# Attention on rows split into fp16 halves, z products ahead of the scan sum, negations on VectorE and ScalarE, and shorter routing chains

## The chip, the cores and the metric

The kernel runs on one core of a Trainium2 chip. The metric is the device time of one launch in microseconds; the median of three runs stands for the kernel. A profiled execution gives the trace, in which PE is TensorE (PEld its weight loads), DVE VectorE, ACT ScalarE, POOL GpSimd and SP SyncE.

## What is computed

Sixteen images of 96 x 96 x 3 become 36 patches and a class row each (37 rows of 256), 128 text rows are appended (165 in all), and two layers follow, each with an attention-like mixer and a mixture of experts, with layer norms and residual sums in f32.

```python
h = _L0_tok_ref(x, ...)                        # patches -> 16 x 37 x 256
h = jnp.concatenate([h, txt], axis=1)          # 16 x 165 x 256
h = h + _L0_attn_ref(_layernorm(h), ...)       # selective scan y, times gelu(z), times W_out
h = h + _L0_ffn_ref(_layernorm(h), ...)        # 8 experts in 4 groups, one group, two experts
h = h + _L1_attn_ref(_layernorm(h), ...)       # rope, causal softmax, one head of 256
h = h + _L1_ffn_ref(_layernorm(h), ...)        # 4 experts, top 2, gelu
# _L1_attn_ref
Q = _rope(x @ Wq.T + bq); K = _rope(x @ Wk.T + bk); V = x @ Wv.T + bv
A = softmax(where(causal, Q @ K.T / sqrt(256), -inf)); return (A @ V) @ Wf.T + bf
# _L1_ffn_ref: the expert sums need c_sum = sum over e of (gelu(b1) @ w2 + b2)
```

## The kernel before

Each engine has one list of instructions that it works off in order, written out by hand; semaphores join the lists. The residual rows stay in SBUF as 16 text tiles of 128 rows and 6 image tiles of three images (111 rows) each, 22 in all.

*Layer 0.* After the patches, TensorE makes three z products (`z_matmul`, two tiles each), then the routing terms, then 60 products on constants that only keep its clock (`keep_clock`), the first output product, and the sum over the scan (`scan_sum`), which waits for the scan on VectorE. From there a z product and an output product (`o_matmul`) alternate, and VectorE adds each output to the rows (L2677) and takes its statistics. Z results go through three PSUM banks to ScalarE's gelu.

*Expert weights of layer 0.* They lie in 24 chunks of 1024 columns. A casting DMA writes the fp16 high half of four chunks at a time; an engine then writes the negated high half into the place of the low half; an accumulating DMA of three chunks adds the f32 weights, so that the low half is left. POOL negates six chunks itself (L2150) and issues all these DMAs, ScalarE negates 18 beside its gelus (L2281).

*Routing* (`positions`, for both layers). On VectorE a chain of small dependent steps, each waiting for the one before, counts tokens per expert and gives each token a slot; TensorE multiplies one-hot matrices (`pe_slots`) to give the source row of each slot (L762) and its destination (L768). POOL gathers the stored rows (L1107, L1311) and adds results back with indirect DMAs. In VectorE's list the experts of lone tiles (L752 to L757) stand between the one-hot matrices and the sources.

*Experts.* Rows and weights are split in fp16 halves; each product is three fp16 products. These stages are left as they are.

*Attention of layer 1* works in f32, one batch after another. TensorE's list in batch b is the following, and `text(b + 2)` waits for ScalarE's normalised rows:

```python
scores(b, slot)
if b < BATCH - 1: project(b + 1, 1 - slot)
if b: values(b - 1, 1 - slot)
if b < BATCH - 2: text(b + 2, slot)
transpose_p(b)
if b < BATCH - 1: text_values(b + 1, 1 - slot)
if b % PER == PER - 1: image_values(b // PER + 1)
```

VectorE's list in batch b is the maxima of the scores, the rotation of the queries of b + 1 (`rope_of(b + 1, 0)`, L1832 and L1834), the reciprocal of the sums, the rotation of the keys, and the addition of the results of b - 1. POOL's list in batch b is the two sums of the rotation (`rope(b + 1)`, L1767), the copy of the image rows of b + 2 (L1762) and the addition of a bias row (L1771). ScalarE's list is the exponents of b, the normalised rows of b + 2 (`norm`, L2171), copies out of PSUM, and a negation of a chunk of layer 1's weights. `scores(b + 1)` (L1540) waits for `rope(b + 1)`. `project` is 8 f32 products with 165 columns (L1513), `text_values` 2 with 264 columns (L1521), `text` 2 transposes (L1501). The f32 products appear in the trace as two instructions each.

*Second routing.* TensorE makes the bias products of four experts (`bias_out`, L1463) and, a second time, their sum over all experts (`biases_sum`, 4 x 24 products, L2002), the last 24 of them after the first transposes of the gathered rows (`meanwhile`).

Of the kernel before, what the change touches and what calls it, by code (L numbers as in the profile page):

```python
# [17 lines left out]
P = 128  # L18
# [6 lines left out]
KC = D // P  # L25
# [52 lines left out]
W0C, CAST, ADDED = XW0 // CW, 4, 3  # L78
BY_ACT = range(6, W0C)
NEGATED = (0, 2, 2, 2, 2, 2, 2, 2, 2, 2, 0)  # L80
# [98 lines left out]
def build(nc, txt, patches, wtok, cols, rows_a, consts, pe_table, wsmall, w0, wattn, rows_f, w1, wsmall1,  # L179
          b2rows, out):  # L180
    with ExitStack() as ctx:
# [145 lines left out]
        xTi = rx.take([KC, IT, P])  # L327
        xTb = rx.take([2, KC, SEQ])
# [13 lines left out]
        rsum = rx.take([2, 2])  # L342

# [26 lines left out]

        def w0_source(first, n):
            return w0[:, first * CW:(first + n) * CW].rearrange("p (c n) -> p c n", n=CW)
# [23 lines left out]
        w0_cast = [sem(f"w0_cast{i}") for i in range(W0C // CAST)]  # L396
        own_negated = sem("own_negated")
        w0_negated = sem("w0_negated")
# [93 lines left out]
        p_exp = sem("p_exp")  # L492
        p_normed = sem("p_normed")
# [7 lines left out]
        rest_ready = sem("rest_ready")  # L501
# [25 lines left out]
        Z_BANKS = (2, 3, 1)  # L527
# [152 lines left out]
        def positions(dve, chain, choices, tiles, done, inrow, intile, pairs, singles):  # L680
# [3 lines left out]
            odd, paired, moved = (sm[:, 12 + 4 * i:16 + 4 * i] for i in (0, 2, 3))  # L684
            so = sm[:, 16:20] if done else sm[:, 28:32]
            if choices == 2:
                chain.link(nc.vector.tensor_tensor(hot, oh[:, 0], oh[:, 1], ALU.add))
                chain.link(nc.vector.tensor_tensor(hot, hot, over(k_valid, 4), ALU.mult))
            else:
                chain.link(nc.vector.tensor_tensor(hot, oh[:, 0], over(k_valid, 4), ALU.mult))  # L690
            nc.vector.tensor_copy(ohb[:, :, :], hot).then_inc(choice_ready, 1)
# [3 lines left out]
            nc.vector.tensor_copy(flat(before_), PS[:, 7, 0:4 * NT])  # L695
            chain.link(nc.vector.tensor_copy(flat(total), PS[:, 7, 128:128 + 4 * NT]))
            chain.link(nc.vector.tensor_tensor_scan(flat(upto), k_reset, flat(total), 0.0, ALU.mult, ALU.add))
# [4 lines left out]
            tl, st, sl = sm[:, 0:4], sm[:, 4:8], sm[:, 8:12]  # L702
# [4 lines left out]
            chain.link(nc.vector.tensor_scalar(sl, st, float(T1), None, ALU.mult))  # L707
            chain.link(nc.vector.tensor_tensor(odd, odd, tl, ALU.subtract))
            chain.link(nc.vector.tensor_scalar(paired, tl, float(T1), None, ALU.mult))
            chain.link(nc.vector.tensor_tensor_scan(so[:, 1:4], onesf[:, 0:3], odd[:, 0:3], 0.0, ALU.mult, ALU.add))  # L710
            chain.link(nc.vector.tensor_scalar(so, so, -1.0, float(2 * pairs + singles - 1), ALU.mult, ALU.add))
            chain.link(nc.vector.tensor_tensor(moved, sl, paired, ALU.add))
            chain.link(nc.vector.scalar_tensor_tensor(out=moved, in0=so, scalar=float(P), in1=moved, op0=ALU.mult,
                                                      op1=ALU.subtract))
            chain.link(nc.vector.tensor_tensor(upto, upto, total, ALU.subtract))
            chain.link(nc.vector.tensor_tensor(before_, before_, upto, ALU.add))
            chain.link(nc.vector.tensor_tensor(upto, before_, over_tokens(paired), ALU.is_ge))
            chain.link(nc.vector.tensor_tensor(upto, upto, over_tokens(moved), ALU.mult))
# [8 lines left out]
            chain.link(nc.vector.tensor_tensor(slots_of, slots_of, k_far.unsqueeze(1).broadcast_to([P, choices, NT]), ALU.add))  # L727
            row_of, first_of = low7[:, 0:choices, :], high7[:, 0:choices, :]
            chain.link(nc.vector.tensor_copy(pos[:, 0:choices, :], slots_of))
# [21 lines left out]
            alone = slice(2 * pairs, 2 * pairs + singles)  # L751
            chain.link(nc.vector.tensor_scalar(sg_, k_slot[:, alone], so[:, 1:2], None, ALU.is_le))  # L752
            for g in (2, 3):
                chain.link(nc.vector.scalar_tensor_tensor(out=sg_, in0=k_slot[:, alone], scalar=so[:, g:g + 1],
                                                          in1=sg_, op0=ALU.is_le, op1=ALU.add))
            chain.link(nc.vector.tensor_tensor(sf[:, alone], sf[:, alone], sg_, ALU.min))
            nc.vector.tensor_copy(slote[:, 0:tiles], sf).then_inc(slots_ready, 1)  # L757
# [10 lines left out]
            nc.vector.tensor_copy(dest[:, 0:tiles], to).then_inc(dest_ready, 1)  # L768
# [4 lines left out]
        def pe_gram(pe):  # L773


            for e in range(G0 * E0):
                for u in range(2):
                    pe.wait_ge(w0_cast[(3 * e + u) // CAST], 16)
# [347 lines left out]
        def pe_experts1(pe, meanwhile):  # L1126
# [42 lines left out]
            def tile(i, slot, j):  # L1169
                w_ = weights(i)  # L1170
                if known(i, 0):
                    transpose_x(0, 0, 0)
                    meanwhile()
# [29 lines left out]
        def act_experts1(act):  # L1203
# [27 lines left out]
            def tile(i, slot, j):  # L1231
                if known(i, 0):
                    split_x(0, 0)
                    act.wait_ge(c_psum, 3)
                    nc.scalar.activation(csum, PS[:, 6, 0:D], ACT.Copy).then_inc(c_copied, 1)
# [9 lines left out]
        def dve_experts1(dve, chain):  # L1245
# [37 lines left out]
            def tile(i, slot, j):  # L1283
# [5 lines left out]
                if known(i, 0):  # L1289
                    dve.wait_ge(c_copied, 2)  # L1290
                    nc.vector.tensor_tensor(rest1[:, :, :], csum.unsqueeze(1).broadcast_to([P, E1, D]), rest1[:, :, :],
                                            ALU.subtract).then_inc(rest_ready, 1)
                if known(i, 1):
                    dve.wait_ge(rest_ready, 1)
# [85 lines left out]
        def pe_rest(pe):  # L1380
# [6 lines left out]
            pe.wait_ge(w0_added, 16 * W0C // ADDED)  # L1387
# [91 lines left out]
        def pe_attention(pe):  # L1479

            def image(n):
                pe.wait_ge(xi_ready, n + 1)
                for k in range(KC):
                    ins = nc.tensor.transpose(PS[:, IMAGE_BANK[n], k * P:(k + 1) * P], xnF[:, 2 + n, k * P:(k + 1) * P],
                                              k_ident)
                ins.then_inc(xi_tr, 1)

            def beside(n):

                pe.wait_ge(xi_ready, n + 1)  # L1490
                for k in range(KC):
                    ins = nc.tensor.transpose(PS[:, 7, BESIDE + k * P:BESIDE + (k + 1) * P], xnF[:, 2 + n, k * P:(k + 1) * P],
                                              k_ident)
                return ins

            def text(b, slot):
                pe.wait_ge(xn_ready, NF + b + 1)
                if not known(b, 0):
                    pe.wait_ge(xTb_copied, b)
                for k in range(KC):  # L1500
                    ins = nc.tensor.transpose(PS[:, 7, k * P:(k + 1) * P], xnF[:, slot, k * P:(k + 1) * P], k_ident)  # L1501
# [4 lines left out]
            def project(b, slot):  # L1506
# [3 lines left out]
                for bank, w_, done in ((0, wq, q_psum), (1, wk, k_psum)):  # L1510
                    for m in range(KC):
                        for k in range(KC):
                            ins = nc.tensor.matmul(PS[:, bank, m * SEQ:(m + 1) * SEQ], w_[:, k, m * P:(m + 1) * P],  # L1513
                                                   xTb[:, slot, k, :], start=(k == 0), stop=(k == KC - 1))
                    ins.then_inc(done, 1)

            def text_values(b, slot):

                wait_from(pe, v_copied, b)
                for k in range(KC):  # L1520
                    ins = nc.tensor.matmul(PS[:, 2, 0:PAYV], xTb[:, slot, k, IMG:SEQ], wvx[:, k, :],  # L1521
                                           start=(k == 0), stop=(k == KC - 1))
                ins.then_inc(v_psum, 1)

            def image_values(n):
# [5 lines left out]
                for k in range(KC):  # L1531
                    ins = nc.tensor.matmul(PS[:, 5, 0:PAYV], xTi[:, k, n, :], wvx[:, k, :], start=(k == 0), stop=(k == KC - 1))
# [79 lines left out]
            keep_clock(8, 5)  # L1612
            project(0, 0)
            keep_clock(16, 5)
            text_values(0, 0)
# [24 lines left out]
        def act_attention(act, roots, normal):  # L1640
            def image(n):
                act.wait_ge(xi_tr, n + 1)
                nc.scalar.activation(xTi[:, :, n, :], PS[:, IMAGE_BANK[n], 0:KC * P].rearrange("p (k r) -> p k r", k=KC),
# [1171 lines left out]
```

## Time and profile before

| | us |
|---|---|
| median of 3 runs | 774.8 (773.57 to 776.81) |
| the profiled execution's own time | 773.13 |
| its span, first to last instruction | 771.3 |
| PE busy | 712.1 (92%) |
| DVE busy | 445.7 (58%) |
| ACT busy | 370.5 (48%) |
| POOL busy | 293.1 (38%) |

The span is read by the stages: front and scan to 100 us, first routing to 138, experts of layer 0 to 338, preparation of attention to 357, attention to 462, second routing to 504, experts of layer 1 to 756, output. The page's line of the granted clock is given in tenths of full speed, which is 2.4 GHz; 0.5 is 1.2 GHz.

### The profile page before, as it was taken

How to read it: one execution, taken by the hardware profiler on the slowest of the kernel's cores; microseconds unless marked ns; L12 is line 12 of the kernel's file. 1: busy time of each engine (PE TensorE's matmuls, PEld its weight loads, DVE VectorE, ACT ScalarE, POOL GpSimd, SP SyncE). 2: the span in 40 equal slices, each digit the busy share in tenths (PEclk: the TensorE clock that was granted, in tenths of full speed). 3: DMA queues.
4: the chain of work that ended last, by engine and by line, in shares of the span. 5: the costliest groups of instructions: out<-in, count | busy, mean ns of one | idle time of the engine just before them, and what ended most of it. 6: DMA issues, size and time to landing. Idle time of an engine off the chain costs nothing.

```text
span 771.3 us, 18265 instructions
## 1 busy us (share of the span) xinstructions
PE 712.1 (92%) x6093; PEld 621.8 (81%) x6094; DVE 445.7 (58%) x1218; ACT 370.5 (48%) x871; POOL 293.1 (38%) x259
## 2 busy tenths in 40 slices
PE   5989985999999999989899999799999999999981
PEld 5768974889888897668789988688888888888871
DVE  5897678344444443437897778745454555555440
ACT  6898745433344433333667656343433444343430
POOL 3348101222333224114455430226555655564331
PEclk9999996999999999999999999899999999999996
DMA  9896998114122112137741279112333332332235
GB/s 273 189 211 81 140 165 265 43 29 120 28 41 41 27 22 35 22 67 193 151 56 18 39 94 316 32 36 43 45 51 55 43 46 48 55 48 41 36 36 154
DMA packets 42214, 66.22 MB, mean 86 GB/s; under 512 B 3680, under 2 KB 29264, under 8 KB 41616
## 3 DMA queue, kind: packets, MB, share of 16 engines
q0 software_dynamic: 22304, 39.19, 33.5%
q1 hardware_dynamic: 19664, 25.93, 10.6%
q8 instruction: 35, 0.57, 0.3%
q10 hardware_dynamic: 192, 0.38, 0.1%
q14 instruction: 19, 0.16, 0.1%
HBM read 65.80 MB, written 23.35 MB: 116 GB/s over the span
## 4 chain that ended last, share of the span: by engine, by line
PE 74%; DVE 13%; ACT 4%; DMA 3%; issue 2%; POOL 1%; POOLq 0%; SPq 0%; DVEq 0%
PE PS L1146 16%; PE PS L1159 15%; PE PS L853 14%; PE PS L890 8%; PE PS L1513 3%; PE PS L868 3%; PE PS L2451 3%; PE PS L2465 2%; ACT Y L2171 2%; PE PS L1540 1%; PE PS L1131 1%; PE PS L1463 1%; DMA xs<-Y 1%; DMA X<-in_w_dram 1%; PE PS L1521 1%
## 5 line engine op out<-in xcount | busy, mean ns | idle before, releaser
L1159 PE MATMUL PS<-X 128*128 x720 | 125.8, 273 | 1.9 <-ACT X L1228 1.9
L1325 POOL DMA_INDIRECT sum<-X,dest x45 | 89.7, 1993 | 96.2 <-ACT X L1228 80.5
L1146 PE MATMUL PS<-X 128*128 128x256 f16 (+1 forms) x768 | 122.7, 265 | 0.7 <-issue 0.7
L1218 ACT ACTIVATE X<-PS,X 128x256 f32<-128x256 f32 (+1 forms) x192 | 72.6, 461 | 103.5 <-PE PS L1146 100.4
L853 PE MATMUL PS<-Y,X 128*128 128x256 f16 x960 | 108.1, 273 | 0.5 <-DVE Y L1022 0.5
L853 PEld LDWEIGHTS PS<-Y,X 128*128 x960 | 93.9, 98 | 11.5 <-issue 0.7
L1146 PE MATMUL PS<-X,Y 128*128 128x256 f16 (+1 forms) x384 | 100.2, 264 | 0.0
L1159 PE MATMUL PS<-Y,X 128*128 x360 | 98.2, 273 | 0.0
L1117 POOL DMA_INDIRECT sum<-Y,dest x24 | 38.6, 1610 | 111.4 <-DVE Y L1050 107.8
L1146 PEld LDWEIGHTS PS<-X 128*128 x768 | 71.7, 97 | 10.6 <-issue 1.3
L1159 PEld LDWEIGHTS PS<-X 128*128 128x128 f16 x720 | 70.4, 98 | 11.1 <-issue 3.0
L1036 DVE TENSOR_TENSOR Y<-PS,Y 128x512 f32<-128x512 f32 x48 | 33.2, 691 | 68.6 <-PE PS L853 48.3
L1311 POOL DMA_INDIRECT X<-xs,source x45 | 45.5, 1010 | 71.2 <-DVE source L762 38.7
L890 PE MATMUL PS<-X,Y 128*128 x576 | 67.5, 273 | 2.0 <-DVE Y L1041 2.0
L890 PEld LDWEIGHTS PS<-X,Y 128*128 128x128 f16 x576 | 56.2, 98 | 8.9 <-issue 2.5
L1277 DVE SCALAR_TENSOR_TENSOR PS<-PS,hscale,X 128x256 f32<-128x256 f32 x45 | 20.0, 488 | 74.9 <-PE PS L1159 74.9
L1269 DVE SCALAR_TENSOR_TENSOR X<-X,hscale 128x1024 f16<-128x1024 f32 (+1 forms) x48 | 58.4, 1217 | 1.7
L974 ACT ACTIVATE Y<-Y,hscale 128x512 f16<-128x512 f32 x40 | 28.9, 722 | 55.7 <-DVE Y L1036 55.7
L1107 POOL DMA_INDIRECT Y<-xs,source x24 | 23.6, 984 | 67.3 <-DMA xs<-Y 33.0
L1041 DVE SCALAR_TENSOR_TENSOR Y<-Y,hscale 128x512 f16<-128x512 f32 x40 | 30.4, 760 | 31.6 <-ACT Y L974 31.6
L1767 POOL TENSOR_TENSOR X<-X 128x330 f32<-128x330 f32 x32 | 28.4, 886 | 50.5 <-DVE X L1834 50.5
L966 ACT ACTIVATE Y<-PS 128x512 f32<-128x512 f32 x48 | 28.3, 589 | 35.8 <-PE PS L853 24.9
(408 smaller groups left out, 1385.3 us busy)
## 6 DMA issues: line engine op xcount, KB each, us to landing
X<-in_w_dram POOLq DMA_DIRECT2D x10, 1024.0 KB, 16.2
X<-in_w_dram POOLq DMA_DIRECT2D x8, 768.0 KB, 15.4
sum<-h SPq DMA_DIRECT2D x2, 2048.0 KB, 15.1
Y<-in_w_dram POOLq DMA_DIRECT2D x4, 1024.0 KB, 11.3
xs<-Y SPq DMA_DIRECT2D x2, 1040.0 KB, 6.2
xs<-Y SPq DMA_DIRECT2D x2, 1032.0 KB, 8.8
h<-in_txt_dram SPq DMA_DIRECT2D x2, 1024.0 KB, 16.5
Y<-in_patches_dram SPq DMA_DIRECT2D x3, 672.0 KB, 7.7
```

What stands on the lines that cost most here:

```text
L853: ins = nc.tensor.matmul(PS[:, 2 * u + half, c * T1:c * T1 + tokens], w_[:, at_:at_ + P], x_[:, slot, k, 0:tokens], start=(n == 0), stop=( ...
L890: ins = nc.tensor.matmul(PS[:, Y_BANKS[s], a * D:(a + 1) * D], h_[:, s, c, a * P:(a + 1) * P], w_[:, at_:at_ + D], start=(c == 0 and n == ...
L974: nc.scalar.activation(to, whole, ACT.Copy, scale=hscale[:, 0:1]).then_inc(hT_hi, 1)
L1036: nc.vector.tensor_tensor(whole, up, gate, ALU.mult).then_inc(h_ready, 1)
L1041: nc.vector.scalar_tensor_tensor(out=low, in0=whole, scalar=hscale[:, 0:1], in1=high, op0=ALU.mult, op1=ALU.subtract).then_inc(hT_lo, 1)
L1117: nc.gpsimd.indirect_dma_start(out=sum0, out_offset=bass.IndirectOffsetOnAxis(ap=dest[:, i:i + 1], axis=0), in_=ybuf[:, u % 2, i - first0( ...
L1146: ins = nc.tensor.matmul(PS[:, 2 * s + c // 2, (c % 2) * T1:(c % 2) * T1 + tokens], part[:, off:off + P], x_[:, slot, k, 0:tokens], start= ...
L1159: ins = nc.tensor.matmul(PS[:, 4 + a, 0:D], h_[:, s, c, a * P:(a + 1) * P], part[:, off:off + D], start=(s == 0 and c == 0 and n == 0), st ...
L1218: ins = nc.scalar.activation(hh1[:, s, c, 0:tokens], PS[:, 2 * s + c // 2, (c % 2) * T1:(c % 2) * T1 + tokens], ACT.Gelu, bias=bias1[:, sl ...
L1269: nc.vector.scalar_tensor_tensor(out=lo_, in0=act_, scalar=hscale[:, 2:3], in1=hi_, op0=ALU.mult, op1=ALU.subtract).then_inc(h1_lo, 1)
L1311: nc.gpsimd.indirect_dma_start(out=x1in[:, u % 2, n - first_tile(u), :], out_offset=None, in_=xs1, in_offset=bass.IndirectOffsetOnAxis(ap= ...
L1325: nc.gpsimd.indirect_dma_start(out=sum1, out_offset=bass.IndirectOffsetOnAxis(ap=dest[:, i:i + 1], axis=0), in_=y1buf[:, u % 2, i - first_ ...
```

## The change

1. *Attention.* The projections of queries, keys and values take rows and weights as two fp16 halves, each f32 product being replaced by three fp16 products. Text rows are split by POOL (`split_text`: a rounding and a subtraction), image rows by VectorE (`norm_image`: two more steps), the query and key weights by ScalarE and VectorE, the value weights by POOL (`split_values`). Transposes are of fp16 halves, four in place of two. `text(b)` on TensorE now waits for `xn_split`. Scores, softmax and values stay in f32.
2. *Layer 0.* `z_matmul(3)` and `z_matmul(4)` stand ahead of the scan sum, with 8 clock-keeping products in place of 60; four z banks at the start; the scan sum goes to another bank and waits for the second gelu; each output product comes a pair earlier against the z products.
3. *Negations of layer 0's weights.* VectorE does 12 (four ahead of its additions of a bias row, eight beside its first four sums), ScalarE 12, POOL none; the accumulating DMAs are of four chunks, six in place of eight; the first casting DMA is issued before a wait of POOL. In layer 1 ScalarE's negations start at b = 2, some batches have two, and POOL's three accumulating DMAs in the loop come at b = 6, 9 and 12.
4. *Routing.* Steps are merged or read PSUM directly; the lone tiles' experts move behind the destinations.
5. *Second routing.* `biases_sum` is gone; VectorE sums the experts' bias products with four additions (`rest_of_outputs`) ahead of the experts; clock-keeping products stand at four places in place of one.

```diff
-BY_ACT = range(6, W0C)
-NEGATED = (0, 2, 2, 2, 2, 2, 2, 2, 2, 2, 0)
+NEGATED1 = (0, 0, 1, 1, 1, 1, 1, 2, 1, 1, 2, 1, 1, 2, 1, 0)
+ADD_IN = (6, 9, 12)
+BY_DVE, BY_ACT = (0, 2, 4), (1, 3, 5)
+BESIDE_GELU = (0, 0, 4, 2, 2, 2, 2)
+BESIDE_SUMS = (2, 2, 2, 2)
...
             def text(b, slot):
-                pe.wait_ge(xn_ready, NF + b + 1)
+                pe.wait_ge(xn_split, b + 1)
...
-                for k in range(KC):
-                    ins = nc.tensor.transpose(PS[:, 7, k * P:(k + 1) * P], xnF[:, slot, k * P:(k + 1) * P], k_ident)
+                for q in range(2 * KC):
+                    ins = nc.tensor.transpose(turned2[:, q * P:(q + 1) * P], xn2[:, slot, q // KC, q % KC * P:(q % KC + 1) * P],
+                                              ident2)
...
                         for k in range(KC):
-                            ins = nc.tensor.matmul(PS[:, bank, m * SEQ:(m + 1) * SEQ], w_[:, k, m * P:(m + 1) * P],
-                                                   xTb[:, slot, k, :], start=(k == 0), stop=(k == KC - 1))
+                            for n, (wh, xq) in enumerate(((0, k), (0, KC + k), (1, k))):
+                                ins = nc.tensor.matmul(PS[:, bank, m * SEQ:(m + 1) * SEQ], w_[:, wh, k, m * P:(m + 1) * P],
+                                                       xTb[:, slot, xq, :], start=(k == 0 and n == 0),
+                                                       stop=(k == KC - 1 and n == 2))
...
+            def split_text(b):
+
+                pool.wait_ge(xn_ready, NF + b + 1)
+                nc.gpsimd.tensor_copy(xn2[:, b % 2, 0, :], xnF[:, b % 2, :]).then_inc(own_rounded, 1)
+                pool.wait_ge(own_rounded, b + 1 + (b > 0))
+                nc.gpsimd.tensor_tensor(xn2[:, b % 2, 1, :], xnF[:, b % 2, :], xn2[:, b % 2, 0, :], ALU.subtract)\
+                    .then_inc(xn_split, 1)
...
+            split_text(0)
             image(0)
+            pool.wait_ge(prep_copied, 4)
+            split_values()
+            split_text(1)
             image(1)
             rope(0)
...
                 if b < BATCH - 1:
                     rope(b + 1)
                 if b < BATCH - 2:
+                    split_text(b + 2)
                     image(b + 2)
                     bias(b + 2)
...
             for i in range(3):
                 z_matmul(i)
             prepare_routes()
-            keep_clock(60, 7)
+            z_matmul(3)
+            keep_clock(8, 5)
             pe.wait_ge(base_ready, 1)
             o_matmul(0)
+            z_matmul(4)
             scan_sum()
-            for i in range(3, NT // 2):
+            o_matmul(1)
+            for i in range(5, NT // 2):
                 z_matmul(i)
-                o_matmul(i - 2)
-            for i in range(NT // 2 - 2, NT // 2):
+                o_matmul(i - 3)
+            for i in range(NT // 2 - 3, NT // 2):
                 o_matmul(i)
...
-            biases_sum(0, True, False)
-            biases_sum(1, False, False)
             biases_rest()
-            keep_clock(85, 3)
+            pe.wait_ge(rows_known, 2)
+            keep_clock(50, 3)
             pe_slots(pe, 1, TOPK * NT, SLOT1, inrow1, intile1)
-            biases_sum(2, False, False)
+            keep_clock(40, 3)
             pe.wait_ge(slots_ready, 2)
             pe.wait_ge(dest_ready, 2)
             pe_scale(pe, 1)
             pe.wait_ge(c_copied, 1)
-
-            def meanwhile():
-                biases_sum(3, False, True).then_inc(c_psum, 1)
-            pe_experts1(pe, meanwhile)
+            keep_clock(45, 3)
+            pe_experts1(pe)
```

## Rows read from the trace of the kernel before

**Rows 1.** The page, part 4: the chain that ended last, by engine

```profile
PE 74%; DVE 13%; ACT 4%; DMA 3%; issue 2%; POOL 1%; POOLq 0%; SPq 0%; DVEq 0%
```

**Rows 2.** Timeline (start us, us, instructions), PE, one batch of attention (b = 10)

```profile
424.35 1.09 PE L1540 MATMUL PS<-X 128*128 128x165 f32 x8
425.28 2.49 PE L1513 MATMUL PS<-X,Y 128*128 128x165 f32 x16
427.61 0.60 PE L1562 MATMUL PS<-X 128*128 128x260 f32 x2
...
428.48 0.38 PE L1501 MATMUL PS<-cst,X 128*128 128x128 f32 x2
428.70 0.27 PE L1550 MATMUL PS<-cst,X 128*128 128x128 f32 x1
...
429.03 1.06 PE L1521 MATMUL PS<-Y,X 128*128 128x264 f32 x4
430.23 1.20 PE L1540 MATMUL PS<-X 128*128 128x165 f32 x8
```

**Rows 3.** Timeline, DVE, the same batch: first and last step of the rotations

```profile
426.69 0.39 DVE L1832 SCALAR_TENSOR_TENSOR X<-PS,ccols,Y 128x165 f32<-128x165 f32 x1 [0.56 <-PE PS L1513]
...
428.83 0.38 DVE L1834 SCALAR_TENSOR_TENSOR X<-PS,ccols,Y 128x165 f32<-128x165 f32 x1
```

**Rows 4.** Timeline, POOL, the same batch: second rotation sum, bias row

```profile
429.29 0.88 POOL L1767 TENSOR_TENSOR X<-X 128x330 f32<-128x330 f32 x1 [0.36 <-DVE X L1834]
...
430.32 0.72 POOL L1771 TENSOR_TENSOR h<-h,wsm 128x256 f32<-128x256 f32 x1
```

**Rows 5.** Timeline, PE: scores of b = 0 and of b = 14

```profile
357.69 1.10 PE L1540 MATMUL PS<-X 128*128 128x165 f32 x8
...
448.68 1.20 PE L1540 MATMUL PS<-X 128*128 128x165 f32 x8
```

**Rows 6.** Chain that ended last, in order of time (start us, us), 455 to 512 us

```profile
470.74 3.57 PE PS L790 x64
...
499.83 3.84 PE PS L2002 x24
503.67 2.63 PE PS L1146 x24
```

**Rows 7.** Timeline, POOL, 0 to 140 us: f32 copy, fp16 negations

```profile
25.96 0.61 POOL L2129 COPY Y<-wsm 128x512 f32<-128x512 f32 x1
...
49.95 8.25 POOL L2150 TENSOR_SCALAR X<-X 128x1024 f16<-128x1024 f16 x3 [5.44 <-DVE Y L2607]
```

**Rows 8.** Timeline, PE, 452 to 512 us: products behind two pauses

```profile
488.42 4.46 PE L590 MATMUL PS<-X 128*128 128x138 bf16 x44 [2.02 <-DVE X L742]
...
498.73 1.10 PE L1131 MATMUL PS<-cst,X 128*128 128x128 f32 x4 [2.14 <-DMA X<-xs,source]
```

**Rows 9.** Windows of 2 us: busy of PE, PEld, DVE, ACT, POOL, then PEclk, DMA share, GB/s

```profile
368.00:370.00 2.00, 0.23 (x2) 0.22 (x3) 0.75 (x4) 1.90 (x8) 0.25 (x1) 1.00 1.15 242
...
486.00:488.00 2.00, 0.41 (x8) 0.23 (x5) 2.00 (x3) 1.53 (x3) 0.00 (x0) 1.00 0.00 0
488.00:490.00 2.00, 1.58 (x15) 1.61 (x16) 2.00 (x3) 0.00 (x0) 0.00 (x0) 0.63 0.00 0
```

**Rows 10.** Chain that ended last, in order of time: one z product

```profile
94.67 1.77 PE PS L2451 x16
```

**Rows 11.** Timeline, DVE: ninth sum, sources of layer 0, one-hot scaling, input split

```profile
101.98 0.48 DVE L2677 SCALAR_TENSOR_TENSOR h<-PS,yv,h 111x256 f32<-111x256 f32 x1 [1.64 <-PE PS L2465]
...
131.05 0.18 DVE L762 SCALAR_TENSOR_TENSOR source<-PS,stats 128x24 uint32<-128x24 f32 x1
...
486.00 0.74 DVE L740 TENSOR_SCALAR X<-X,cst 128x2024 bf16<-128x2024 bf16 x1
...
500.50 0.69 DVE L1250 TENSOR_TENSOR X<-PS,X 128x512 f16<-128x512 f32 x1 [4.57 <-ACT X L1207]
```

**Rows 12.** Timeline, POOL: first gather of layer 0

```profile
132.10 1.09 POOL L1107 DMA_INDIRECT Y<-xs,source  x1 [33.03 <-DMA xs<-Y]
```

More of the change, by code:

```diff
@@ L342, in build @@
         rsum = rx.take([2, 2])
+        xn2, xi2 = rx.take([2, 2, D], F16), rx.take([2, 2, D], F16)
+        wqk2 = stage[:, 1, :].bitcast(F16).rearrange("p (h n) -> p h n", h=2)
+        wq2, wk2 = (wqk2[:, :, i * KC * D:(i + 1) * KC * D].rearrange("p h (k n) -> p h k n", k=KC) for i in range(2))
+        wvx2 = wqk.bitcast(F16)[:, 0:2 * KC * PAYV].rearrange("p (h k n) -> p h k n", h=2, k=KC)
+        ident2 = stage[:, 0, CW - P // 2:CW].bitcast(F16)
+        turned2 = PS[:, 7, :].bitcast(F16)
         rg = Region(X, XE)
@@ L767, in positions @@
             dest_of_token(dve, chain, tiles, from_, to, taken)
-            nc.vector.tensor_copy(dest[:, 0:tiles], to).then_inc(dest_ready, 1)
+            chain.link(nc.vector.tensor_copy(dest[:, 0:tiles], to))
+            dve.sem_inc(dest_ready, 1)
+            alone = slice(2 * pairs, 2 * pairs + singles)
+            chain.link(nc.vector.tensor_scalar(so[:, 1:4], so[:, 1:4], -1.0, float(last), ALU.mult, ALU.add))
+            chain.link(nc.vector.tensor_scalar(sg_, k_slot[:, alone], so[:, 1:2], None, ALU.is_le))
+            for g in (2, 3):
+                chain.link(nc.vector.scalar_tensor_tensor(out=sg_, in0=k_slot[:, alone], scalar=so[:, g:g + 1],
+                                                          in1=sg_, op0=ALU.is_le, op1=ALU.add))
+            chain.link(nc.vector.tensor_tensor(sf[:, alone], sf[:, alone], sg_, ALU.min))
+            nc.vector.tensor_copy(slote[:, 0:tiles], sf).then_inc(slots_ready, 1)
         def pe_gram(pe):
@@ L1697, in negate @@
             def negate(b):
-                for n in range(b + 1 if b else 0, min(b + 2, W1W // CW)):
+                for n in range(sum(NEGATED1[0:b]), sum(NEGATED1[0:b + 1])):
                     act.wait_ge(*w1_landed(n * CW // W1N))
@@ L1804, in pool_attention @@
                     image_bias(IMAGE_BIAS.index(b))
-                if b and b % (W1N // CW) == 0:
-                    add(b * CW // W1N - 1)
+                if b in ADD_IN:
+                    add(ADD_IN.index(b))
             add(E1 - 1)
@@ L1987, in act_layer1 @@
                 .then_inc(c_copied, 1)
+            act_rows(act, 1, inrow1)
             act_experts1(act)
@@ L1994, in pe_layer1 @@
             pe.wait_ge(small1_loaded, 16)
-            def biases_sum(e, first, last):
-                for c in range(F1 // P):
-                    off = e * W1N + KC * F1 + c * D
-                    for n, (g_, w_) in enumerate(((gbh, w1h), (gbh, w1l), (gbl, w1h))):
-                        left = g_[:, e * (F1 // P) + c:e * (F1 // P) + c + 1].broadcast_to([P, P])
-                        ins = nc.tensor.matmul(PS[:, 6, 0:D], left, w_[:, off:off + D], start=(first and c == 0 and n == 0),
-                                               stop=(last and c == F1 // P - 1 and n == 2))
-                return ins
             def biases_rest():
@@ L2691, in _ @@
                     add_bout(BATCH, IT)
+                for _ in range(BESIDE_SUMS[i] if i < len(BESIDE_SUMS) else 0):
+                    negate(chunks.pop(0))
                 if i == BATCH // 2 - 1:
```

215 lines of the change are left out of this document (118 added, 97 removed).

## Prediction

> **What bounds the kernel now.** I read the shares of the chain that ended last first: TensorE (PE) carries 74% of the span, VectorE (DVE) 13% [rows 1]. The two expert stages, 138 to 333 us and 504 to 756 us, are gapless PE work that the change doesn't touch, so whatever it brings or costs lies in three stretches: layer 0's z and output products with the first routing (54 to 138 us), attention (340 to 462 us), and the second routing (462 to 504 us). Within attention I then read one undisturbed batch, b = 10, engine by engine [rows 2 to 4], and the distance of the first from the last scores that open a full cycle [rows 5]: 14 cycles in 448.68 - 357.69 = 91.0 us, 6.5 us each. The undisturbed one takes 430.23 - 424.35 = 5.88 us. The remaining 91.0 - 14 x 5.88 = 8.7 us are image products and DVE statistics in some of them. PE looks full in such a cycle, but what ends last is a loop through other engines. Let S be the start of the projections, 425.28 [rows 2]. DVE takes up the rotation of the queries at 426.69, 0.24 us after the first half of the projections (1.17 us), and ends that of the keys at 429.21 [rows 3]; POOL adds from 429.29 to 430.17 [rows 4]; the next scores start at 430.23, released by nothing else. So the loop is scores 0.93, then 4.95 us from S to the next scores, and PE's last piece (the text values, from 429.03 for 0.89) is done 0.3 us before.
>
> **Attention: the new order of waits.** The change takes away PE time. The price of an fp16 product follows from 64 of 128 columns in 3.57 us (56 ns each, own weights for each) and 24 of 256 columns in 2.63 us (110 ns) [rows 6]: 71 ns for 165 columns, some 113 ns for 264. The projections become 24 x 71 ns = 1.71 us instead of 2.33 [rows 2], their first half 0.86 instead of 1.17; the text values 6 x 113 ns = 0.68 instead of 0.89; the four fp16 transposes stay at 0.22 us. The Trainium skill (TensorE: Matmul & The Clock Gate, section Back-to-back issue gap) gives 81 ns to a sustained pair of weight load and 128-column product. The row of 64 says 56 ns, and I go by it; by the page an estimate of the first half is at least 0.97 us, which adds 0.11 us to a cycle and 1.6 us in all.
>
> It also adds a step to POOL, and the place of this step decides. In POOL's list, split_text(b + 2) stands behind rope(b + 1); in PE's list, text(b + 2) waits for that split, and behind text(b + 2) are queued transpose_p(b), text_values(b + 1) and scores(b + 1). In the kernel before, text(b + 2) waited only for ScalarE's normalised rows, ready long before. Now scores(b + 1) can't start at the end of POOL's rotation any more: first come POOL's rounding and subtraction, then PE's transposes and the values. The subtraction of 256 elements costs 0.72 us as in [rows 4]. A rounding of 256 elements from f32 to f16 has no row on POOL; below it is the f32 copy of 512 elements (0.61 us, so 0.3 for half of it), above it the f16 TENSOR_SCALAR of 1024 at 8.25 / 3 = 2.75 us (0.69 for a quarter) [rows 7]; I take 0.4, nearer to the copy, and 0.05 for the wait between the two. So the loop after is, from S:
> - first half of the projections 0.86, to DVE 0.24, both rotations with the quotients between them 429.21 - 426.69 = 2.52, to POOL 0.08, sum 0.88: 4.58;
> - split 0.4 + 0.05 + 0.72 = 1.17, to PE 0.05: 5.80;
> - transposes 0.22, transposes of p 3 x 0.11 = 0.33, text values 0.68, scores 0.93: 7.96.
>
> Against 5.88 this is 2.08 us more in each of the 14 cycles that have a split (b = 0 to 13), 14 x 7.96 = 111.4 in all. Four image products (0.68 each) and four more image transposes (0.22 each) now lie behind the split too: +3.6. DVE's statistics are covered by the longer loop except in the two cycles with a full Newton chain, and ScalarE's three double negations may delay an exponent: +2. Sum 117 against 91.0: **+26 us**. The last cycle has no split and gains from the shorter projections: -0.5. Ahead of the first scores, two image splits on DVE and the split of two text rows and of the value weights on POOL stand in line before project(0) and rope(0): about 1.3 us later. The split of the query and key weights is hidden, since both engines wait there for the transposed weights.
>
> **The clock.** With 1.71 + 0.88 of values behind S, PE has no work from S + 2.6 to S + 5.8: 3.2 us of idle time in one piece in each cycle. Twice in this trace the engine stood still for about 2 us: 2.02 before 488.42 and 2.14 before 498.73 [rows 8]. After the first the clock granted fell from 1.00 to a mean of 0.63 in the next stretch of 2 us, so to the 1.2 GHz level in most of it [rows 9]; the second shows in the durations below. A pause of 1.8 us in 368 to 370 left it at 1.00 [rows 9]. A pause of 3.2 us is longer than the one that cost the clock, so I expect the fall in most cycles. What it costs: 24 products of 256 columns took 3.84 us after the second pause, and 2.63 us at 2.4 GHz [rows 6]: 1.2 us. The ends are 0 (the 368 us row) and 2.16 us (everything behind the pause, scores included, at half speed). 14 x 1.2 = **+17 us**, between 0 and +30.
>
> **Layer 0.** Two z products, 1.77 us each [rows 10], move from behind the scan sum to before it, where clock-keeping products stood: -3.5. Their order also brings the last three output products together, so that DVE's wait of 1.64 us before the ninth [rows 11] goes: -1.6. Negations: POOL's six go. DVE gets twelve; 16-bit in and out costs 0.74 us for 2024 elements [rows 11], so about 0.4 for 1024. Eight lie two by two in waits of 1.6 us like that one; four stand ahead of the step that prepares the scan, where DVE waits for ScalarE in part: +0.5, between 0 and 1.6. Then the routing: five short DVE steps (copies, a multiply, an add, a rounding) leave the chain, and six on the lone tiles move behind the destinations; at some 0.2 us each, like the step at 131.05 that gives the sources [rows 11], these come 2.3 us earlier besides. Gathering waits today for the stored rows (132.10 [rows 12]); with six adds issued sooner, I expect the store to come as early as the sources. Sum about **-7**, with -4 if the store stays the later one and -8 at best; who is late next is PE's scale with its clock-keeping products, some 0.2 us behind.
>
> **Second routing.** The sums of four experts' bias products, 96 in all, leave PE. Only the last 24 stood on the chain: 3.84 us from 499.83 on [rows 6]. In their place stand 18 clock-keeping products (1.0 us at 56 ns), and what ends last is then the input split, done at 500.50 + 0.69 = 501.19 [rows 11], 1.4 us after the transposes: -2.4. DVE's shorter chain brings the sources about 1.4 us earlier; the four DVE adds that replace the products fit while it waits for the gathered rows. Clock-keeping products ahead of the gathered rows can use up some of it. Together **-4**, between -2 and -5.
>
> **Sum.** -7 + 1.3 + 26 + 17 - 0.5 - 4 = +33 (32.8). The span of 771.3 becomes 804; the profiled run itself, 773.13, lies 1.7 under the median 774.8, to which I add the rounded 32: **806 us**.
>
> **Rivals.**
> - *The clock holds.* For it: the row at 368 us, and that the pause lies between two stretches of dense work. Against it: the row at 488 us, with a shorter pause. Without the 17: **790 us**.
> - *All behind the pause at half speed*, and the rounding at 0.69: 14 x (0.96 + 0.3) = 17.6 more: **823 us**. For it: two of two long pauses cost the clock at once; against it: there, part of what followed was fast again.
> - *Faster: the split costs PE no wait.* The place is PE's wait at text(b + 2). If the split were done by the time PE gets there, S + 2.6, for which POOL has idle time ahead of the rotation sums, the loop would be 5.88 - 0.31 = 5.57; 14 of them, with today's extras of 8.7 less 0.7 for smaller products, make 86, that is -5; without a pause the clock holds: 774.8 - 7 + 1.3 - 5 - 0.5 - 4 = **760 us**. The other parts sum to -10.2, so it decides from (91.0 + 10.2) / 14 = 7.23 us a cycle, extras of 0.4 included, or a loop of 6.8, and with the clock up: nearly all of the split's 1.17 us would have to vanish. Against it: POOL's list is in order, and the rotation stands ahead.
> - *The change does less than it says*, for instance if the projections don't get shorter by 0.3 us in the first half: +4, inside the forecast.
>
> **How the numbers follow.** Forecast (loop of 8 us and more, clock falling) 0.56, 806; clock holds 0.20, 790; half speed throughout 0.10, 823; split hidden 0.11, 760; all cancelled within 0.5% 0.03. The range takes in the bounds of the clock and of the rounding: 786 to 824; outside it remain the hidden split and little else. A difference of 0.5% (3.9 us) is about what a measurement of this kernel can tell from none: faster 0.11, same 0.03, slower 0.86.
>
> **What will show it.** In the profile after: starts of scores 8 us apart or more for b = 0 to 13 and some 5.5 for the last; before the text transposes an idle time of about 3 us each, released by POOL's subtraction; a PEclk below 1.0 in the slices of attention; at PE the last z product ahead of the eighth output product; sources of both layers earlier by the amounts above. I am wrong if PE's idle time in these batches stays under 1 us, or if it is released by ScalarE.

## The result and the profile after

The changed kernel takes 819.0 us (816.69 to 821.19) against 774.5 us (773.57 to 776.81) for the kernel before in the same comparison: a ratio of 1.0577, with a 95% interval of 1.0557 to 1.0597. The forecast was 806 us with a range of 786 to 824, so sign and range held and the size was 13 us short. The profiled execution took 819.52 us, its span is 817.7.

Five marks of the trace, read in the same views of both kernels, split the span into stages; the column "added" says how much longer each stage got (us):

| up to | before | after | added | forecast |
|---|---|---|---|---|
| first expert product of layer 0 | 138.51 | 139.25 | +0.7 | -7 |
| scores of b = 0 | 357.69 | 362.32 | +3.9 | +1.3 |
| scores of b = 14 | 448.68 | 498.13 | +44.8 | +26 and +17 |
| first expert product of layer 1 | 503.67 | 550.20 | -2.9 | -0.5 and -4 |
| end | 771.3 | 817.7 | -0.1 | 0 |

The loss is attention, and it came nearly as worked out (44.8 for 43). What the forecast missed lies around it: 7.7 us of gain in layer 0, 2.6 us of loss ahead of attention, 1.6 us of gain behind it. These three and the 1.8 us of the loop are 13.7 us, the whole difference between the forecast span (804) and the measured one.

The scores of b = 0 and b = 14 on TensorE in the changed kernel (start us, us, instruction), to be set beside [rows 5]:

```profile
362.32 2.07 PE L1557 MATMUL PS<-X 128*128 128x165 f32 x8 [1.93 <-POOL X L1789]
...
498.13 1.09 PE L1557 MATMUL PS<-X 128*128 128x165 f32 x8
```

The 14 cycles take 135.8 us, 9.7 each. One of them, b = 10, on TensorE (compare [rows 2]):

```profile
460.69 1.47 PE L1557 MATMUL PS<-X 128*128 128x165 f32 x8
461.99 1.90 PE L1526 MATMUL PS<-X,stage 128*128 128x165 f16 x24
...
464.21 0.60 PE L1580 MATMUL PS<-X 128*128 128x260 f32 x2
467.69 0.40 PE L1512 MATMUL PS<-stage,X 128*128 128x128 f16 x4 [2.88 <-POOL X L1796]
...
468.25 1.50 PE L1536 MATMUL PS<-Y,X 128*128 128x264 f16 x6
469.55 2.01 PE L1557 MATMUL PS<-X 128*128 128x165 f32 x8
```

and on POOL (compare [rows 4]):

```profile
464.42 0.88 POOL L1789 TENSOR_TENSOR X<-X 128x330 f32<-128x330 f32 x1 [3.35 <-DVE X L1878]
465.66 0.88 POOL L1789 TENSOR_TENSOR X<-X 128x330 f32<-128x330 f32 x1 [0.36 <-DVE X L1878]
466.49 0.39 POOL L1794 CAST X<-X 128x256 f16<-128x256 f32 x1
466.96 0.67 POOL L1796 TENSOR_TENSOR X<-X 128x256 f16<-128x256 f32 x1
```

TensorE stands still for 2.88 us ahead of the text transposes, and POOL's subtraction (L1796) releases it. The rounding took 0.39 us (forecast 0.4), the subtraction 0.67 (0.72). From the projections to the text transposes it is 467.69 - 461.99 = 5.70 us; the sum in the prediction said 5.80.

The clock in the same cycle, in stretches of 2 us (busy of PE, PEld, DVE, ACT, POOL, then PEclk, DMA share, GB/s; compare [rows 9]):

```profile
464.00:466.00 2.00, 0.81 (x4) 0.36 (x2) 2.00 (x9) 0.76 (x2) 1.22 (x2) 1.00 1.12 138
466.00:468.00 2.00, 0.31 (x5) 0.32 (x6) 0.74 (x5) 0.00 (x0) 1.92 (x5) 1.00 1.06 136
468.00:470.00 2.00, 2.00 (x13) 1.65 (x12) 0.00 (x0) 1.22 (x5) 0.57 (x1) 0.57 1.10 142
470.00:472.00 2.00, 2.00 (x15) 2.00 (x14) 0.33 (x2) 2.00 (x4) 0.00 (x0) 0.58 0.13 15
```

In this pause the granted clock reads 1.00 (2.4 GHz); it falls to 0.50 (1.2 GHz) about 0.5 us behind it. So the four transposes still run fast here (0.40 us, against 0.61 at 458.32, where the clock was already down), and the six text values take 1.50 us (0.84 in b = 13, at 497.46) and the next eight score instructions 2.01 (1.09).

Layer 0, the chain that ended last, in order of time (start us, us, what):

```profile
109.00 9.84 ACT Y L2213 x20
...
119.43 12.27 DMA xs<-Y
...
136.22 1.12 PE PS L853 x4
137.33 1.92 PE PS L572 x18
139.25 0.85 PE PS L871 x4
```

and the same view of the kernel before:

```profile
113.52 9.84 ACT Y L2171 x20
...
123.37 8.26 DMA xs<-Y
...
138.51 5.41 PE PS L853 x48
```

ScalarE is 4.5 us earlier with the scaled rows, as the forecast had it. But their last store takes 12.27 us in place of 8.26 and lands at 131.70 us, where it landed before (131.63). The sources, at 131.05 before [rows 11], now come at 124.15, on VectorE:

```profile
124.15 0.18 DVE L771 SCALAR_TENSOR_TENSOR source<-PS,stats 128x24 uint32<-128x24 f32 x1
```

Before, POOL's first gather started 1.05 us behind them (132.10 [rows 12]); now it starts 7.8 us behind them, released by the store:

```profile
131.97 1.10 POOL L1125 DMA_INDIRECT Y<-xs,source  x1 [44.22 <-DMA xs<-Y]
```

So nothing of the 4.5 us came through. TensorE now waits 6.46 us for the gathered rows (up to 136.22), and the clock is down behind it (0.50 from 135 to 140 us, 1.00 before): the four transposes take 1.12 in place of 0.67 us, and the 18 clock-keeping products 1.92 us (107 ns each), which is 0.4 us more than the input split behind the transposes needed before. These two are the 0.7 us that were lost.

Ahead of attention, on VectorE and POOL:

```profile
348.23 0.75 DVE L1854 BATCH_NORM_STATS2 stats<-h 128x6 f32<-128x256 f32 x2 [1.14 <-DMA h<-sum]
...
355.08 1.05 DVE L2565 TENSOR_TENSOR rs<-rs 128x17 f32<-128x17 f32 x1
...
358.18 0.29 DVE L1867 CAST X<-X 128x256 f16<-128x256 f32 x1
358.51 0.42 DVE L1868 TENSOR_TENSOR X<-X 128x256 f16<-128x256 f32 x1
```

```profile
354.89 1.21 POOL L1804 TENSOR_TENSOR Y<-Y 128x528 f16<-128x528 f32 x1
```

The first statistics come 209.0 us behind the first expert product (before: 345.93 - 138.51 = 207.4), as VectorE now waits for the rows that SP loads back: +1.6. Two image splits of 0.75 us: +1.5. One VectorE step of 17 elements takes 1.05 us, where the same step took 0.18 at 349.72: +0.9. Together 4.0, for 3.9 measured.

Second routing, the chain in order of time:

```profile
545.73 2.51 PE PS L572 x45
548.24 0.46 PE PS L1149 x4
...
550.20 2.80 PE PS L1164 x24
```

The first gather is issued at 542.09 and, at the 4.15 us that it took before from POOL's start to its landing (494.53 to 498.68), landed at about 546.2. The transposes start 2.0 us later, behind 45 clock-keeping products.

### The profile page after: what moved, and what is told of

It is laid out like the page before. It is cut to its first block, busy times and chain, and to the rows that moved or that the text cites. A ratio compares the mean times of both kernels' runs of the same rounds, so it can differ in the third digit from the quotient of the medians.

```text
span 817.7 us, 18586 instructions
## 1 busy us (share of the span) xinstructions
PE 708.6 (87%) x6229; PEld 618.5 (76%) x6230; DVE 456.8 (56%) x1235; ACT 370.7 (45%) x867; POOL 291.3 (36%) x285
## 3 DMA queue, kind: packets, MB, share of 16 engines
q1 hardware_dynamic: 19664, 25.93, 10.1%
## 4 chain that ended last, share of the span: by engine, by line
PE 72%; DVE 12%; ACT 6%; DMA 4%; POOL 3%; issue 2%; POOLq 0%; SPq 0%; DVEq 0%
PE PS L1164 15%; PE PS L1177 15%; PE PS L871 13%; PE PS L908 8%; PE PS L1526 3%; PE PS L886 3%; PE PS L1557 2%; PE PS L2509 2%; PE PS L1536 2%; PE PS L2495 2%; POOL X L1789 2%; DMA xs<-Y 1%; ACT Y L2213 1%; DVE X L1876 1%; DVE X L1878 1%
## 5 line engine op out<-in xcount | busy, mean ns | idle before, releaser
L871 PEld LDWEIGHTS PS<-Y,X 128*128 x960 | 94.4, 98 | 11.2
L1789 POOL TENSOR_TENSOR X<-X 128x330 f32<-128x330 f32 x32 | 28.2, 882 | 75.5 <-DVE X L1878 75.5
L572 PE MATMUL PS<-onesb 128*128 128x128 bf16 x415 | 31.8, 247 | 16.2 <-DVE rc L747 9.4
```

The lines of the kernel that those rows point to most:

```text
L572: nc.tensor.matmul(PS[:, bank, 0:P], onesb[:, :], onesb[:, :], start=True, stop=True)
L871: ins = nc.tensor.matmul(PS[:, 2 * u + half, c * T1:c * T1 + tokens], w_[:, at_:at_ + P], x_[:, slot, k, 0:tokens], start=(n == 0), stop=( ...
L1789: nc.gpsimd.tensor_tensor(qkT[:, b % 2, i], tcos[:, i], tsin[:, i], ALU.add).then_inc(rope_done, 1)
```

## The experiments

### The place of the split

```diff
                 for b in range(BATCH):
+                if b < BATCH - 2:
+                    split_text(b + 2)
                 if b < BATCH - 1:
                     rope(b + 1)
                 if b < BATCH - 2:
-                    split_text(b + 2)
                     image(b + 2)
```

Alone, this is the first run; the second has in ScalarE's list `norm(b + 2)` ahead of `exps(b)` besides.

> Only POOL's list is changed: split_text(b + 2) ahead of rope(b + 1). ScalarE's rows stay behind the exponents, where they are done 2.4 us after the start of the projections. Theory (place of the split): POOL splits from 2.5 to 3.6 us after that start, TensorE's wait for it shrinks from 2.9 to about 0.9 us, the clock stays up, and the two rotation sums come behind it, the second at 5.35 us: loop 5.4 + 0.93 = 6.35 us, some 95 us between the scores of b = 0 and b = 14, about 778 us in all. Rival (cost of the split itself): above 8.4 us a cycle and 800 us.

Measured: 786.1 us, one execution. 14 cycles in 464.29 - 363.58 = 100.7 us, 7.2 each (95 were expected). A plain cycle takes the 6.4 us that were worked out; b = 2 and b = 6 take 11.2 and 9.6.

```profile
363.58 1.85 PE L1557 MATMUL PS<-X 128*128 128x165 f32 x8 [1.93 <-POOL X L1789]
...
464.29 1.20 PE L1557 MATMUL PS<-X 128*128 128x165 f32 x8 [0.28 <-POOL X L1789]
```

> In POOL's list split_text(b + 2) stands ahead of rope(b + 1), and in ScalarE's list the normalised rows of b + 2 stand ahead of the exponents of b; nothing else differs from the changed kernel. Theory (place of the split): the split is done before TensorE gets to the text transposes, its wait of about 2.9 us per batch goes, and with it the fall of the granted clock. The loop is then that of the rotation, 4.6 us from the projections to the next scores and 0.93 for the scores, 5.6 us; 14 of them with about 8 us of image products and statistics are 86 us in place of 135.8 between the scores of b = 0 and b = 14, and the run takes about 819 - 50 = 769 us. Rival (cost of the split itself, wherever it stands: more POOL work and more TensorE instructions in each batch): the cycles stay above 8.4 us and the run above 800. Second rival: the rows ahead of the exponents delay these and the products behind them, loop about 6.5 us, 95 us in all, 778 us.

Measured: 774.7 us, a ratio to the kernel before of 1.0021 (1.0006 to 1.0036). Scores on TensorE:

```profile
362.12 1.20 PE L1557 MATMUL PS<-X 128*128 128x165 f32 x8 [1.21 <-POOL X L1789]
...
447.94 1.20 PE L1557 MATMUL PS<-X 128*128 128x165 f32 x8
453.59 1.20 PE L1557 MATMUL PS<-X 128*128 128x165 f32 x8 [0.56 <-POOL X L1789]
```

The same work in another order is 44 us faster: the 14 cycles take 91.5 us, and scores are again released by the rotation sum (L1789). So the place of the split is the cause, and the rival (its cost wherever it stands) falls. POOL's order alone brings 35 of the 44 us (the run before this one); ScalarE's order by itself was not run. But 86 were expected. A plain cycle is 5.65 us, nearly as worked out, so the second rival (6.5 us) falls too; the rest, 91.5 - 14 x 5.65 = 12.4 us, is more than the 8.7 before. It sits in cycles with VectorE's image rows, now three steps each: b = 2, 6 and 7 take 10.0, 8.2 and 7.7 us (8.6, 6.8 and 6.0 before). In b = 2 TensorE still waits 1.8 us for the split, and in all three it waits for ScalarE's normalised probabilities, whose exponents wait for VectorE's maxima:

```profile
417.26 0.33 PE L1567 MATMUL PS<-cst,X 128*128 128x128 f32 x1 [1.63 <-ACT X L1691]
```

### The clock

```diff
                 if b < BATCH - 2:
+                    for _ in range(40):
+                        nc.tensor.matmul(PS[:, 4, 3 * P:4 * P], onesb[:, :], onesb[:, :], start=True, stop=True)
                     text(b + 2, slot)
```

> The changed kernel with 40 clock-keeping products of 128 columns on TensorE ahead of each text(b + 2), in a part of PSUM that nothing reads; the split keeps its place. At 56 ns each they fill 2.2 of the 2.4 to 3.2 us that TensorE waits there, so they delay nothing. Theory: the wait stays as the profile of the changed kernel shows it, but the granted clock stays at 1.00, and each cycle loses the part that came from the clock: 14 cycles fall from 135.8 to about 117 us (8.4 us each), and the run takes about 800 us. Rival (the slow products behind the pause have another cause than the pause, or the lower clock costs nothing on the path): the 14 cycles stay within 3 us of 135.8 and the run within 3 us of 819.

Measured: 801.6 us, one execution. A cycle, and the whole of the 14:

```profile
401.09 2.40 PE L1647 MATMUL PS<-onesb 128*128 128x128 bf16 x40
404.14 0.40 PE L1512 MATMUL PS<-stage,X 128*128 128x128 f16 x4 [0.66 <-POOL X L1798]
...
404.71 0.84 PE L1536 MATMUL PS<-Y,X 128*128 128x264 f16 x6
```

```profile
363.75:480.35 116.60, 105.66 (x1290) 98.71 (x1291) 77.70 (x313) 60.22 (x204) 63.78 (x99) 1.00 0.39 62
```

The split still releases the transposes, the clock is 1.00 throughout (0.84 on the mean in the changed kernel), and the cycles fall from 135.8 to 116.6 us. A plain cycle takes 7.88 us, for 7.96 in the prediction's sum. So the 44.8 us are 116.6 - 91.0 = 25.6 for the wait and 19.2 for the clock; the forecast had 26 and 17. The rival (the clock costs nothing on the path) falls.

### The rest of the change alone

Attention as in the kernel before (f32, no split), all else as changed.

> The changed kernel with attention as it was before (f32 projections and values, no splits); layer 0, negations, both routings as changed. Theory: the parts add up as the two traces say, stage by stage: layer 0 and first routing +0.7 us, second routing -2.4 us, attention as before: 774.5 - 1.7 = about 773 us, no difference that can be measured. Rival (interaction): two negations of layer 1's weights in some batches on ScalarE delay exponents in an f32 attention that has no slack for them, 2 to 4 us more: 775 to 777 us.

Measured: 770.3 us, a ratio of 0.9971 (0.9959 to 0.9984). So by the two ratios attention costs 47 us and the rest gains 2.2. On the same chip the changed kernel with the split first took 774.7 us, 4.5 more than the f32 one: with 4.5 of the 41.5 us of TensorE's wait in the 14 cycles left, the split attention doesn't pay here. Whether it would with none left was not run. The f32 cycles:

```profile
361.68 1.10 PE L1550 MATMUL PS<-X 128*128 128x165 f32 x8
...
450.60 1.20 PE L1550 MATMUL PS<-X 128*128 128x165 f32 x8
```

88.9 us for 14, 2.1 less than before. Within these cycles only the places of ScalarE's negations (none in b = 0 and 1) and of POOL's accumulating transfers differ, so the rival (negations delay exponents) falls too. The other stages come to no gain in this profiled execution (771.6 us of span, 771.3 before); it was the longest execution of ten, by 3.6 us over their median, and the stages don't show where the median gains.

### The stores of layer 0

In the changed kernel, from 96 to 114 us (queue: packets, MB, share of 16 engines) the accumulating transfers take most of the engines' time; from 114 to 132 it is SP's queue:

```profile
q0 software_dynamic: 1076, 2.14, 91.6%
q1 hardware_dynamic: 769, 0.79, 15.7%
```

```profile
q1 hardware_dynamic: 4943, 5.00, 88.5%
```

SP's queue has 2816 KB of residual rows ahead of 2838 KB of scaled rows, and of the former only 0.79 MB are through by 114 us. The residual rows aren't needed before 163 us.

```diff
-            for t, n in ((0, BATCH), (BATCH, IT)):
-                ... sp.dma_start(sum0[...], h[...])
             for t, n in ((0, 8), (8, 8), (BATCH, IT)):
                 ... sp.dma_start(xs0[...], pay[...])
+            for t, n in ((0, BATCH), (BATCH, IT)):
+                ... sp.dma_start(sum0[...], h[...])
```

> The changed kernel with one exchange in SP's list: the three stores of the scaled rows (xs), for which the first gather waits, stand ahead of the two stores of the residual rows (sum, 2.75 MB), for which only the first addition of results waits. In the profile of the changed kernel the scaled rows are ready 4.5 us earlier than before, but their last store takes 12.3 instead of 8.3 us and lands at 131.7 us as before. Theory (SP's queue works its stores off in order, and 2 MB of the residual rows are still ahead when the accumulating transfers end at 115 us): the store lands at 125 to 127 us, and the first expert product of layer 0 starts at about 134 instead of 139.3, so the run takes about 814 us. Rival (the accumulating transfers of the expert weights hold the engines until then, whatever the order on SP's queue): the store lands at 131 us or later and the run stays at 819. Second rival: the residual rows then lie beside the first gathers, which take 2 us longer, and half of the gain goes.

Measured: 817.0 us (808.33 to 818.55), a ratio of 1.0524 (1.0461 to 1.0587), which can't be told from 1.0577. The stage can:

```profile
119.50 6.06 DMA xs<-Y
...
127.24 6.55 DMA Y<-xs,source
...
136.12 3.89 PE PS L871 x26
```

The store lands at 125.56 us, as expected from the order on the queue; the gather then takes 6.55 us in place of 2.81, so that 3.1 of 6.1 us are left. The second rival was right about that part.

> The changed kernel with attention in f32 as it was before, and SP's stores of the scaled rows ahead of those of the residual rows. Theory (order on SP's queue): 5 us below the same kernel without the exchange, 770.3 - 5 = about 765 us. Rival (accumulating transfers): 770 us.

Measured: 766.8 us, ratio 0.9917 (0.9898 to 0.9937): 3.5 us below the same kernel without the exchange, or 4.2 by the two ratios, as the two ran on different chips; 5 were expected.

> The kernel before with the exchange of stores alone. There the scaled rows land at 131.63 us and the sources of the first gather come at 131.23 us, so two waits end nearly together. Theory (two limits in series: the change shortened the chain to the sources, the store kept the gather where it was): the store lands 4 us earlier, the first gather starts at most 0.4 us earlier, and as it then has the residual rows beside it, the first expert product comes 1 to 3 us later than at 138.5: 774 to 777 us. Rival (the store alone was the limit in both kernels): the first product comes 3 us earlier, 771 us.

Measured: 775.5 us, ratio 1.0023 (1.0008 to 1.0039): slower by 0.2%, as expected. The chain:

```profile
131.31 0.20 DVE source L762
...
133.76 4.62 DMA Y<-xs,source
...
140.57 1.48 PE PS L853 x12
```

In the kernel before, the sources were as late as the store. The exchange alone gains nothing there, and the longer gather costs 2 us. Two limits ended together; the change moved one, the exchange the other, and in layer 0 each alone is worth nothing. By the ratios the change without the split attention gains 2.2 us, the exchange alone loses 1.8, and both together gain 6.4.

### The clock-keeping products of the second routing

```diff
-            keep_clock(45, 3)
+            keep_clock(8, 3)
             pe_experts1(pe)
```

> The changed kernel with 8 instead of 45 clock-keeping products ahead of the first transposes of layer 1's experts. In its profile these 45 start behind a wait of 2.3 us and take 2.5 us, and the transposes start at 548.2, about 2 us after the gathered rows landed. Theory (the products themselves are what ends last): the transposes start when the rows land, 2 us earlier against the one-hot products; as the clock is then still down, they take 1.1 instead of 0.5 us, and the first expert product comes about 1.4 us earlier against the one-hot products. Rival (the products pay for themselves): the expert's first 24 products then run at half clock, 3.8 instead of 2.8 us, and the second unit starts no earlier than now. In the time of the run that is 819 against 818, so the stage tells it.

Measured: 820.4 us, one execution. Counted from the one-hot products (535.61 here, 536.27 in the changed kernel), the transposes come at 10.1 instead of 12.0 us, but the second unit at 554.25 - 535.61 = 18.6 instead of 553.43 - 536.27 = 17.2:

```profile
546.21 1.24 DVE X L2115
...
549.25 4.57 PE PS L1164 x24
```

VectorE's four additions for the bias products, ending at 547.45, now hold up the input split, and the first 24 products take 4.57 us in place of 2.80. Here the products paid for themselves.

> As the kernel with f32 attention and the exchanged stores, and with 8 instead of 45 clock-keeping products ahead of the transposes of layer 1's experts; with f32 attention those 45 took 4.1 us, all of it at half clock. Theory: 2 to 3 us less than with 45, about 762 us. Rival (the products pay for themselves): 765 us or above.

Measured: 764.4 us, ratio 0.9896 (0.9868 to 0.9925). The interval overlaps with the kernel with 45, so the expected 2 to 3 us are not shown by the times. From the last scores to the second unit it is 48.2 us against 50.2, and the first 24 products took 2.80 us in both, so in these two profiled executions the products did not pay. The same 45 products took 2.51 us in the changed kernel, 3.78 with the exchanged stores and 4.09 with f32 attention (91 ns each, so not all of it at half clock, as was expected: that is 107); what sets this was not found, and the question of their best number stays open.

### A faster kernel

The kernel of the run before, in which SP in addition waits for the first gathers:

```diff
+            sp.wait_ge(x_in[0], 32)
+            sp.wait_ge(x_in[1], 32)
             for t, n in ((0, BATCH), (BATCH, IT)):
                 ... sp.dma_start(sum0[...], h[...])
```

> The kernel with f32 attention, exchanged stores and 8 kept products; in addition SP issues the stores of the residual rows only when the first four gathers have landed (they are needed by about 159 us). With the stores exchanged, the scaled rows landed at 124.8 us, but the first gather then took 6.2 us in place of 2.8. Theory (the residual rows share the engines with the gather): the gather takes 2.8 to 3 us again, the first expert product of layer 0 starts at 132 to 133 instead of 135.8, and the run takes about 761 us. Rival (something else slows the gather, such as the last accumulating transfers): it still takes 6 us, and the run stays at 764.

Measured: 761.4 us (760.27 to 766.29), ratio 0.9847 (0.9831 to 0.9862): the fastest, 1.5% below the kernel before. Gathers from 120 to 150 us (KB each, median us from issue to landing), first without that wait, then with it:

```profile
Y<-xs,source POOLq DMA_INDIRECT x7, 5.1
```

```profile
Y<-xs,source POOLq DMA_INDIRECT x7, 2.8
```

The residual rows were what slowed the gather. The profiled execution is the longest of the five, its sources came 3.4 us later than in the run before (127.44 for 124.05), and its first expert product (136.92) says nothing on the 132 to 133 expected, which stay unshown.

## Why the prediction was right, and where it was short

- **What bounds attention, and the loop after.** Right, step by step: the wait for POOL's subtraction, 5.70 us for 5.80 from the projections to the transposes, and +25.6 for +26 at full clock. The order in POOL's list was the cause, as moving it showed.
- **The clock.** Right in the mechanism: the clock fell in 11 of the 14 cycles ("in most cycles"), and taking the fall behind the pause of 2.02 us at 488 us rather than none behind that of 1.8 us at 368 us was the right choice of row. That the size is so near, 19.2 us for 17, is partly luck: the sum had 14 falls of 1.2 us, and the runs show 11, of 1.7 us on the mean.
- **Layer 0: the step that failed.** "With six adds issued sooner, I expect the store to come as early as the sources", and with it -4 "if the store stays the later one". The first part of the sum held (4.5 us to the scaled rows for 3.5 + 1.6 - 0.5 = 4.6, and 6.9 us to the sources). But the bound was wrong: it took the store's length as fixed and let its end move with its start. The DMA engines were full from 80 to 130 us in both kernels (share 1.03 to 1.09 in every stretch of 5 or 10 us) with the same transfers, so with the stores in this order the end did not move (131.69 for 131.63 us); with the rows stored first it came at 125.56. The bound should have been 0, which is what the 4.5 us were worth. That the last add was issued 12 us sooner (86.0 for 97.8) brought nothing: the adds now took up to 30.9 us to landing, before up to 19.0.
- **Ahead of attention.** A term too small (3.9 for 1.3). The two image splits were there (1.5); the wait for the rows (1.6) and the slow step (0.9) were not.
- **Second routing.** -2.4 for -4, with the -0.5 of the last cycle as forecast. The sources came 1.4 us earlier as said (0.3 us between the one-hot products and them, 4.81 for 5.11, and 1.1 us ahead of the one-hot products). The step "what ends last is then the input split, 1.4 us after the transposes" holds, but the transposes themselves were held by 45 products, which was named and not priced; and the additions do not quite "fit while it waits for the gathered rows", as the run with fewer products shows.
- **The rival at 760.** Its mechanism was built (the split mostly hidden), and the run took 775. The loop came 5.5 us longer than its 86 through VectorE's image rows, and it carried the same -7, +1.3 and -4.
- **The sum.** It comes to 32.8 us and was added to 774.8 as 32. With 32.8 the forecast is 807.6, so 1.6 of the 13 us is a slip of the adding.

## What to carry to other kernels

A step added to an in-order list delays all that waits behind it on other engines: the same split made 14 cycles 45 us longer behind the rotation, 10 us longer ahead of it, and 0.5 us longer when its input was moved ahead too. So ask of each added step whether its inputs are ready before those of its neighbours. Where the DMA engines were already full, a store issued 4 us sooner ended no sooner; what moved its end by 6 us was what stood ahead of it in its queue. So store first what somebody waits for. Where two waits end together, shorten both or neither.

## What was not expected of the hardware

The price of a pause is paid by what stands behind it, and not each pause has the same price. In b = 10 the granted clock reads 1.00 in a pause of 2.9 us and falls when work has resumed (1.00 from 466 to 468 us, 0.57 from 468 to 470). Of the 14 pauses of the changed kernel's loop, five (2.44 to 4.12 us long) end with the clock at 0.50 already and the transposes at 0.61 us; behind six (2.44 to 2.89 us) it falls 0.5 to 1.5 us after the transposes start; behind three (2.85 to 2.90 us, ahead of 381.17, 439.24 and 496.89) it stays at 1.00 up to the next pause. So in this range the length of a pause alone doesn't tell what it costs.

A VectorE step of 17 elements took 1.05 us instead of 0.18. It starts at 355.08 and ends at 356.13, while POOL's subtraction runs from 354.89 to 356.10. The Trainium skill (SBUF — State Buffer, section Who interferes with whom) says that a VectorE instruction with two SBUF inputs contends with a GpSimd instruction that reads SBUF; it calls the port pair that the two share an exclusive lock, and says that the order of issue decides which is blocked. This row agrees: VectorE starts second, and its end lies 0.03 us behind POOL's. A step with one SBUF input, at 354.47 us, also took 0.37 instead of 0.18 us and ended 0.03 us behind POOL's rounding (354.81). No run here took either apart.
